# A decoder block on one core: scatters paced by TensorE's signals, the exponential in two halves, first scores ahead of the last shifted scores

## What is computed

```python
x = x + linear_attention_and_ffn(layernorm(x))        # 16 heads, elu + 1 features, then a GELU FFN
x = x + cross_attention(layernorm(x), ctx)            # 16 heads of 8, 77 keys per sequence, softmax
x = x + experts(layernorm(x))                         # 8 experts, top 2, capacity 1280 rows per expert and slot
```

## Time and profile before

| | us |
|---|---|
| median of three runs | 974.47 |
| lowest and highest | 972.26, 980.99 |
| the profiled execution's own time | 977.34 |
| its span, first to last instruction | 975.5 |
| TensorE busy (matmuls) | 844.6 |
| VectorE, GpSimd, ScalarE busy | 641.7, 539.9, 453.3 |

### The profile page before, as it was taken

How to read it: one execution, slowest core, us unless ns; L and a number is a source line. 1 busy time by engine, 2 the same in 40 slices (tenths; PEclk the granted TensorE clock), 3 DMA queues, 4 the chain that set the end, 5 groups by cost and what they waited for, 6 DMA issues and landing times.

```text
span 975.5 us, 25508 instructions
## 1 busy us (share of the span) xinstructions
PE 844.6 (87%) x9107; PEld 625.8 (64%) x9107; DVE 641.7 (66%) x2064; ACT 453.3 (46%) x708; POOL 539.9 (55%) x747
## 2 busy tenths in 40 slices
PE   4799999999999999999999999862789889979883
PEld 3577787787667776666766667741456656656661
DVE  5888988988567877777777776734244544434443
ACT  1466766766367666666666655521222222222220
POOL 3465665665532366666655655565356656565565
PEclk8899999999999999999999998955799999989997
DMA  6369930000000011110000000100433344546440
GB/s 234 98 238 390 388 123 0 0 1 1 1 2 14 25 58 57 57 41 31 28 28 30 28 30 26 55 29 32 156 106 131 115 134 108 157 126 198 135 154 3
DMA packets 50336, 87.01 MB, mean 89 GB/s; under 512 B 12809, under 2 KB 28105, under 8 KB 50232
## 3 DMA queue, kind: packets, MB, share of 16 engines
q1 hardware_dynamic: 37872, 72.18, 22.0%
q0 software_dynamic: 11264, 12.70, 4.0%
q10 hardware_dynamic: 1096, 0.73, 0.2%
HBM read 42.08 MB, written 58.41 MB: 103 GB/s over the span
## 4 chain that ended last, share of the span: by engine, by line
PE 48%; DVE 8%; another core or an unknown queue 8%; issue 7%; ACT 3%; POOL 2%; DMA 1%; DVEq 0%; SPq 0%; POOLq 0%; ACTq 0%
PE psum L1398 6%; PE psum L1418 6%; PE psum L1880 6%; PE psum L1383 5%; PE psum L1892 5%; PE psum L1388 3%; PE psum L1429 2%; PE psum L1401 2%; DVE h L1832 2%; PE psum L1365 2%; DVE yo L1817 2%; PE psum L1369 1%; ACT num L1269 1%; PE psum L626 1%
## 5 line engine op out<-in xcount | busy, mean ns | idle before, releaser
L1779 POOL DMA_INDIRECT out<-yo,token x160 | 158.7, 992 | 123.3 <-issue 108.4
L852 POOL DMA_INDIRECT dispatched<-z,idx x128 | 129.6, 1013 | 72.7 <-issue 47.0
L1261 ACT ACTIVATE PT<-psum,key_bias 77x2048 f32<-77x2048 f32 x64 | 125.5, 1961 | 74.9 <-PE psum L1401 74.9
L1861 ACT ACTIVATE act_g<-psum 128x512 f32<-128x512 f32 x80 | 46.1, 596 | 191.2 <-DVE h L1832 95.3
L1398 PE MATMUL psum<-qT,Kb 32*77 32x128 f32 x2048 | 126.8, 282 | 0.8 <-issue 0.8
L951 DVE TENSOR_REDUCE top_score<-psum 128x8 f32<-128x616 f32 x128 | 101.6, 794 | 29.7 <-PE psum L1383 27.2
L1817 DVE SCALAR_TENSOR_TENSOR yo<-psum,xin,base 128x128 f32<-128x128 f32 x156 | 44.0, 343 | 111.6 <-remote 65.6
L1892 PE MATMUL psum<-down,h 128*128 128x128 f32 x640 | 85.5, 290 | 28.9 <-DVE h L1832 24.8
L1383 PE MATMUL psum<-Kb,qT 32*128 32x308 f32 x512 | 101.5, 471 | 0.8 <-ACT z3T L1252 0.4
L1892 PEld LDWEIGHTS psum<-down,h 128*128 128x128 f32 x640 | 80.0, 203 | 33.9 <-DVE h L1832 29.3
L1401 PE MATMUL psum<-MT,minus_sel 32*77 32x128 bf16 x1024 | 97.3, 217 | 2.3 <-issue 2.3
(11 more groups left out here) (177 smaller groups left out, 1743.5 us busy)
## 6 DMA issues: line engine op xcount, KB each, us to landing
dispatched<-zeros SPq DMA_DIRECT2D x40, 522.0 KB, 7.3
xin<-dispatched SPq DMA_DIRECT2D x40, 522.0 KB
out<-zeros SPq DMA_DIRECT2D x20, 256.0 KB, 3.1
first<-out SPq DMA_DIRECT2D x20, 256.0 KB
X<-in_x SPq DMA_DIRECT2D x16, 256.0 KB, 2.6
out<-X SPq DMA_DIRECT2D x16, 256.0 KB
out<-yo,token POOLq DMA_INDIRECT x160
ctx<-in_ctxT SPq DMA_DIRECT2D x4, 616.0 KB, 6.3
```

The costliest lines, as they stand in the source:

```text
L852: pool.indirect_dma_start(xg[k], bass.IndirectOffsetOnAxis(ap=idx[n % Z4][:, t, k:k + 1], axis=0), z4[n % Z4][:, t, :], None, bounds_check ...
L1261: nc.scalar.activation(PT[j % 2][:], T.rearrange("p a c -> p (a c)"), ACT.Exp, bias=key_bias[:, bass.ds(b, 1)]).then_inc(s["PT_ready"], 1)
L1779: pool.indirect_dma_start(rows_out if slot else out, bass.IndirectOffsetOnAxis(ap=token[i][:, t:t + 1], axis=0), yo[i][:, t, :], None, bou ...
```

## The change

Four things:
- *GpSimd in cross attention.* The first scatter of step j waits for T_ps of this batch's last shifted scores, the second for OT_ps (the turned numerators of batch b - 1) and no more for MT_ps. The bias add moves from step 2 to step 3. In `last` each scatter of group 13, and each second one of group 14, gets a wait for a TensorE signal.
- *GpSimd in the experts.* Each of the four scatters of tile n waits for one signal of tile m = n + 2: its first gate projection, the transposes that follow it, the down projection, the first up projection. Tiles 18, 19 and 37 to 39 are left as they are.
- *ScalarE.* `exps` is two instructions of 1024 columns, each behind its half of T_ps; TensorE's waits for PT_ready count two for each batch.
- *TensorE.* The first scores of batch b + 2, with their waits, come inside `shifted`, ahead of its steps 4 and 5. Steps 0 and 1 wait for the first half of the exponential of batch b - 1, the others for the second.

```diff
@@ gpsimd, steps @@
                     if group(n):
+
                         if j == 0:
                             scatter_ready(n)
+                        pool.wait_ge(s["T_ps"], 4 * b + 4)
                         scatter_rows(n, j, 0)
...
-                    if j == 2:
+                    if j == 3:
                         add_out_bias(g)
                     if group(n):
-                        if batch(b + 1):
-                            pool.wait_ge(s["MT_ps"], b + 2)
+                        pool.wait_ge(s["OT_ps"], b)
                         scatter_rows(n, j, 1)
@@ gpsimd, last @@
-                for u in range(G4):
-                    for k in range(K2):
-                        scatter_rows(NG - 3, u, k)
+                pool.wait_ge(s["T_ps"], 4 * NB)
+                scatter_rows(NG - 3, 0, 0)
+                pool.wait_ge(s["z4T_ps"], NG - 1)
+                scatter_rows(NG - 3, 0, 1)
+                pool.wait_ge(s["pv_ps"], 8 * (NB - 1))
+                scatter_rows(NG - 3, 1, 0)
+                pool.wait_ge(s["gate_ps"], NG - 1)
+                scatter_rows(NG - 3, 1, 1)
+                pool.wait_ge(s["OT_ps"], NB - 1)
+                scatter_rows(NG - 3, 2, 0)
+                pool.wait_ge(s["pv_ps"], 8 * NB)
+                scatter_rows(NG - 3, 2, 1)
+                pool.wait_ge(s["OT_ps"], NB)
+                scatter_rows(NG - 3, 3, 0)
+                pool.wait_ge(s["oT_ps"], NG)
+                scatter_rows(NG - 3, 3, 1)
+
                 ln_scale(NG - 1, 4, mom4, var4, rs4, shift4)
-                for n in (NG - 2, NG - 1):
-                    scatter_ready(n)
...
+                scatter_ready(NG - 2)
+                scatter_rows(NG - 2, 0, 0)
+                scatter_rows(NG - 2, 1, 0)
+                pool.wait_ge(s["z4T_ps"], NG)
...
+                pool.wait_ge(s["gate_ps"], NG)
...
+                pool.wait_ge(s["rank_ps"], NG)
...
@@ scalar @@
             def exps(b, j):
-                act.wait_ge(s["T_ps"], 4 * b + 4)
                 if some(b - 1):
                     act.wait_ge(s["pv_ps"], 8 * (b - 1))
-                nc.scalar.activation(PT[j % 2][:], T.rearrange("p a c -> p (a c)"), ACT.Exp,
-                                     bias=key_bias[:, bass.ds(b, 1)]).then_inc(s["PT_ready"], 1)
+                for half in range(2):
+                    act.wait_ge(s["T_ps"], 4 * b + 2 * half + 2)
+                    nc.scalar.activation(PT[j % 2][:, half * HB * 2 * P:(half + 1) * HB * 2 * P],
+                                         T[:, 2 * half:2 * half + 2, :].rearrange("p a c -> p (a c)"), ACT.Exp,
+                                         bias=key_bias[:, bass.ds(b, 1)]).then_inc(s["PT_ready"], 1)
@@ tensor @@
-            def shifted(g, par, b, j):
+            def shifted(g, par, b, j, beside):
 
                 if some(b):
-                    pe.wait_ge(s["PT_ready"], b)
+                    pe.wait_ge(s["PT_ready"], 2 * b - 1)
                 pe.wait_ge(s["MT_ready"], b + 1)
                 for step in range(HB + 2):
+                    if step == 2 and some(b):
+                        pe.wait_ge(s["PT_ready"], 2 * b)
+                    if step == HB:
+                        beside()
...
-                pe.wait_ge(s["PT_ready"], b + 1)
+                pe.wait_ge(s["PT_ready"], 2 * b + 2)
...
+                    if batch(b):
+                        shifted(g, par, b, j, first_scores)
@@ gpsimd, experts @@
+                    m = n + 2
+                    paced = m < NE - 1 and n not in (SECOND - 2, SECOND - 1)
                     for t in range(G4):
+                        if paced and t == 0:
+                            pool.wait_ge(s["gate_ps"], HC * m + 1)
+                        if paced and t == 1:
+                            pool.wait_ge(s["xT_ps"], m + 2)
+                        if paced and t == 2:
+                            pool.wait_ge(s["y_ps"], m)
+                        if paced and t == 3:
+                            pool.wait_ge(s["up_ps"], HC * m + 1)
```

19 lines of the change are left out of this document (13 added, 6 removed).

## The result

The changed kernel takes 977.77 us (median of 20 runs, 970.35 to 985.6), the kernel before beside it 972.59 us (20 runs, 966.02 to 982.18). The ratio is 1.005, interval 1.0026 to 1.0075: half a per cent slower, where 931.5 us and a gain of 4% were forecast. The profiled execution took 981.43 us, its span is 979.6 us.

A forecast was written before the change was run, and what follows sets the result against it. TensorE's signals held beside GpSimd's scatters were taken as the bound. Terms 27 (experts) + 14 (attention) + 0 + 0 + 2 (end) = 43 us off 977.34 gave 934.3, with the runs' median 2.9 lower 931.5 us; range 903 to 965.

The forecast's parts named there:

- rival 1: Both stages and end of attention: all holds of TensorE's signals go, 75 us won, 899 us; chance 0.15.
- Rival 4: Whole kernel: nothing is held, late starts have another cause, pacing does nothing, 974.5 us; chance 0.05.
- The bias add (1.28 us) moves one step on: Attention, GpSimd: the add moves into a step without GpSimd layer norm; no term of its own in the sum.
- the slower one: Experts: held signals space scatters 1.9 us apart, a tile takes 7.6 us, 993 us in all; chance 0.08.
- Attention's scatters, 14 us: Attention groups: pacing wins half of 2.1 us, 1.1 us a group over 13 groups; bounds 28 and -20.
- My lower bound: Attention's scatters: -20 us, the split late by 0.8 us in two steps of each group, nothing won.
- rival 2: Holds meet other signals in attention, nothing won; expert scatters run in rows again, 6.2 us a tile; 956 us; chance 0.17.
- Experts, 27 us: Expert stage: a wait ahead of each scatter in 35 of 40 tiles wins 27 us; bounds 39 and -33.
- Of the 39 us I keep 12 as not won: Experts: 5 us for unpaced tiles, 4 for catching up in the second slot, 3 for 0.1 a paced tile.
- End of attention, 2 us: Last scatters: six still run in a row beside the last batch; gain 2 us, bounds -5 and 10.
- Exponential and first scores, 0: Attention: exponential halves worth 0; first scores start VectorE's second maximum 0.4 us earlier, counted in the scatters' 1.1 us.
- the marks I had set: Signs of right: gate projections 5.7 to 6.1 us, unknown-queue share more than halved, groups near 22.9, remote waits mostly gone.

The follow-up runs named there:

- e1: Changed kernel with the bias add back in step 2, against the kernel before: 957.22 us against 978.46, ratio 0.978.
- e17: Changed kernel with the bias add back in step 2, second time, against the kernel before: 963.07 us against 979.99, ratio 0.985.
- e13: Kernel before with only the two waits ahead of the attention steps' scatters, against the kernel before: ratio 1.000.
- e14: Kernel before with only the waits among the last scatters of the attention stage, against the kernel before: ratio 0.995.
- e4: Kernel before with only the exponential in halves and first scores ahead of the last two shifted-score steps, against the kernel before: 972.4 us, ratio 0.995.
- e8: Changed kernel with attention steps' scatters unpaced and bias add in step 2, against the kernel before, on a chip without holds: ratio 0.999.
- e11: Changed kernel with attention steps' scatters unpaced and bias add in step 2, against the kernel before, on a chip with holds: ratio 0.983.

## Why the prediction was wrong

**What bounds the kernel: right, on this chip.** TensorE's signals are held beside a scatter; on B, with the same scatters and no holds, the groups and tiles are the free ones of the earlier trace rows. The price that I read off, 2.1 us a group and 1.0 a tile, 75 us in all in rival 1, is what the kernel before takes less on B: 901.6 us against 972.6 to 980.6. Rival 4 (nothing is held) falls for this chip; on B nothing is held, and pacing does nothing (0.999).

**The failed step: "The bias add (1.28 us) moves one step on, into a step where GpSimd has no layer norm."** I asked what it meets on GpSimd and not on VectorE. It meets the routing multiply, 1.85 us in 11 groups, and comes to 20 to 26 us (e1 and e17 against the changed kernel: 0.978 and 0.985 against 1.005). At the full clock it is 1.1 to 1.5 us a group (24.9 to 25.0 us against 23.5 and 23.8 in e1 and e17), and the rest comes with the lower clock of the changed kernel's groups. The step had no term in my sum. What I had on the ports that the two engines share I used for rival 4 alone. None of my rivals held this, and the slower one (GpSimd's rate in the experts) was another mechanism; it did not occur.

**Attention's scatters, 14 us: nothing (e13).** "so in step 3 the split, not a hold, decides, some 0.5 us after where it would be without any scatter" was right in kind; the split came 0.93 us later and the step took 0.6 more; what failed is "I take half of the 2.1 us". Of step 0's gain of 0.91 us steps 3 and 2 spend 0.73; the 0.2 us that are left are within the noise of the groups. My lower bound described it ("the split late by 0.8 us in two steps of each group, nothing won"); rival 2 (the holds move) is what happened here.

**Experts, 27 us: 15.4.** Mis-sized was "Of the 39 us I keep 12 as not won"; it is 24, and 9 to 16 us were won over the runs (6.25 to 6.45 us a tile). All 39 were not to be had: on B, without holds, the tile is 5.73 to 5.81 us. Timeline of the changed kernel, a delayed tile outside the second slot:

```profile
784.56 0.97 POOL L1827 DMA_INDIRECT out<-yo,token  x1 [1.94 <-PE psum L1922]
...
788.92 1.95 PE L1940 MATMUL psum<-down,h 128*128 128x128 f32 x16
...
790.94 0.97 POOL L1827 DMA_INDIRECT out<-yo,token  x1 [0.30 <-issue]
793.21 1.13 DVE L1865 SCALAR_TENSOR_TENSOR yo<-psum,xin,base 128x128 f32<-128x128 f32 x4 [4.83 <-remote]
...
795.59 2.05 PE L1940 MATMUL psum<-down,h 128*128 128x128 f32 x16 [0.84 <-issue]
```

Six scatters from 784.56 to 790.94, about 1.28 us apart: the first still waited for its signal, the five behind it found theirs past, since GpSimd is late, and VectorE starts 2.27 us after the last one (2.29 in the earlier trace rows). "No scatter starts before a signal has come through, so a run cannot hold them for longer than the scatters in flight" is true only while GpSimd is not behind, and it falls behind in ordinary tiles, not only at the second slot.

**End of attention, 2 us: 4 to 5 (e14).** Within the bounds, and the mechanism was right: scatters still run in a row beside the last batch, and its numerators still wait 4.88 us. **Exponential and first scores, 0: about 5 together (e4)**, of which 1.3 us can be pointed at in the trace; what the first scores win I had booked under the scatters' 1.1 us. Two halves of the exponential take 2.11 us back to back, one whole 1.96, as reckoned (2.10).

**The sum.** The parts that were tried alone multiply to 0.990 x 0.995 x 0.995 x 1.000 = 0.980, and the kernel which has them all gives 0.978 (e1) and 0.985 (e17). So without the bias add's move it would have been about 951 to 958 us, inside the range, though with half or less of the 43 us forecast; the move turned it into 1.005. Of the marks I had set, the chain's share of another core or an unknown queue fell from 7.9 to 3.8%, as for "right". VectorE's remote waits ahead of yo fell from 65.6 to 36.8 us, so they are not "mostly gone"; gate projections 5.7 to 6.1 us apart (they are 6.28) and groups near 22.9 us (they are 26.0) did not come.

## What to carry to other kernels

When an instruction is moved to fill a gap on its engine, look at what the other engines run there, and of GpSimd and VectorE above all: here a four-element operation of 0.16 us became 2.0 ahead of GpSimd's add of 128x512, and what it cost depended on what was queued behind it. A change of several edits, each harmless alone, can lose by two of them together (here paced scatters took away the wait that had covered the collision), so time them singly and in pairs. Compare groups at the same granted clock: the place of the first scores looked like 0.2 us on B and was 0.01. Pacing by named signals helps only an engine that is on time; one that has fallen behind finds them past and runs as before.

## What the runs showed of the hardware

The same program takes 901.6 us on one chip and 972.6 to 980.6 on the others, and nearly the whole difference lies where GpSimd issues scatters. In one kernel traced on both kinds (e8 and e11, spans of 901.1 and 962.1 us) the groups take 21.68 and 23.92 us, the end of attention 54.7 and 58.6, the tiles 5.81 and 6.42, and the stretch without scatters 14.9 in both. On the slow ones TensorE's signals are held beside a scatter, by 0.6 to 0.8 us in the rows shown; on the quick one they arrive after 0.09 us at the median. Why chips differ was not found out. That kernel's gain from avoiding holds, 17.5 us on C (0.983), is nothing on the quick chip (0.999).

A VectorE instruction on a few elements in SBUF waits for GpSimd's tensor_tensor of 128x512 even though it began 0.7 us ahead of it by the rows, when that one is next behind a scatter and the instruction starts 0.33 us or more after the scatter's start; the statistics of the layer norm do not wait there, and the scatter alone (e1, L1099 at 0.16 us) does not hold L1099.
